# Repeating softmax denominators by DMA and moving residual sums into a wait, in a fused attention and expert kernel

## The reference

```python
x = x + attn(layernorm(x))          # c_kv = x@W_DKV; k = c_kv@W_UK; v = c_kv@W_UV; q = x@W_UQ
                                    # ctx = softmax(causal(q k^T / 4)) v ; ctx @ W_O
h = layernorm(x)
logits = h @ Wr / temp; topw, topi = top_k(logits, 2); topw = softmax(topw)
for e in range(8):
    a, g = split(h @ W1[e] + b1[e]);  y = a * silu(g) @ W2[e] + b2[e]
    out += y * sum(where(topi == e, topw, 0))
x = x + out
```

## Time and profile before

| what | us |
|---|---|
| median of 3 runs | 1150.02 (1148.51 to 1151.36) |
| the profiled execution | 1161.29 |
| its span, first to last instruction | 1159.5 |
| PE busy, in the span | 1044.3 (90%) |
| DVE busy | 762.8 (66%) |
| ACT busy | 503.1 (43%) |
| POOL busy | 411.0 (35%) |

### The profile page before, as it was taken

One profiled execution on the slowest core, in us unless ns is written; L12 is line 12 of the kernel. 1 busy time (PEld: TensorE's weight loads), 2 busy tenths in 40 slices (PEclk: granted clock), 3 DMA queues, 4 the chain that ended last, 5 costly groups with the idle time before them and its releaser, 6 DMA issues. The chain is left out here.

```text
span 1159.5 us, 19495 instructions
## 1 busy us (share of the span) xinstructions
PE 1044.3 (90%) x5364; PEld 549.1 (47%) x5365; DVE 762.8 (66%) x2270; ACT 503.1 (43%) x1060; POOL 411.0 (35%) x781
## 2 busy tenths in 40 slices
PE   5998999999999999999877730899999999999995
PEld 2443333333333333335546630466666666666663
DVE  3776999999999898896435432455555555555552
ACT  2553377777777777775343330122222222222221
POOL 5566233333333333342263345022222222222222
PEclk9997599999999999999797755899999999999998
DMA  2869766665555444414238573122222222222222
GB/s 88 261 229 264 140 129 131 133 131 129 120 120 121 85 84 85 84 41 123 92 102 299 193 234 110 35 45 46 47 45 45 45 45 45 45 45 45 45 45 27
DMA packets 102395, 121.22 MB, mean 105 GB/s; under 512 B 26352, under 2 KB 81776, under 8 KB 102320
## 3 DMA queue, kind: packets, MB, share of 16 engines
q1 hardware_dynamic: 89024, 102.55, 35.1%
q0 software_dynamic: 13296, 17.77, 9.0%
HBM read 70.27 MB, written 49.63 MB: 103 GB/s over the span
## 5 line engine op out<-in xcount | busy, mean ns | idle before, releaser
L740 ACT ACTIVATE b_prob<-bank 128x512 f32<-128x512 f32 (+3 forms) x768 | 312.8, 507 | 91.2 <-PE bank L784 90.7
L766 PE MATMUL bank<-b_k_st,b_q_st 96*128 96x512 bf16 (+3 forms) x768 | 255.6, 346 | 5.5 <-DVE b_neg_max L694 1.7
L694 DVE CUSTOM_DVE_ANT_0 bank<-bank,b_mask_max 128x256 f32<-128x256 f32 (+3 forms) x512 | 241.2, 507 | 24.5 <-PE bank L766 24.4
L652 POOL TENSOR_SCALAR_AFFINE_SELECT b_prob<-b_prob 128x128 f32<-128x128 f32 x512 | 145.9, 294 | 307.1 <-ACT b_prob L740 302.4
L784 PE MATMUL bank<-b_q_st,b_k_st 99*128 99x512 bf16 (+3 forms) x768 | 245.5, 335 | 3.2 <-ACT b_prob L740 1.1
L1644 POOL DMA_INDIRECT out_dram<-e_y,e_token x71 | 110.7, 1560 | 325.0 <-DVE e_y L1698 313.7
L697 DVE TENSOR_REDUCE b_neg_max<-bank 128x1 f32<-128x512 f32 x256 | 175.6, 686 | 13.6 <-PE bank L766 11.1
L805 PE MATMUL bank<-b_prob,b_v_aug 128*32 128x512 f32 (+3 forms) x1536 | 145.8, 498 | 0.0
L1768 PE MATMUL e_y_ps<-w_sb,e_hiddenT 128*128 x568 | 134.4, 379 | 1.8 <-ACT e_hiddenT L1721 1.8
L1751 PE MATMUL e_g_ps<-w_sb,e_rowsT 128*128 x284 | 135.4, 599 | 0.4 <-issue 0.4
L1751 PE MATMUL e_a_ps<-w_sb,e_rowsT 128*128 x284 | 133.4, 592 | 0.0
(11 more groups left out here) (172 smaller groups left out, 1007.6 us busy)
## 6 DMA issues: line engine op xcount, KB each, us to landing
w_sb<-in_L_ffn_W SPq DMA_DIRECT2D x12, 1024.0 KB
e_rows<-slot_rows SPq DMA_DIRECT2D x72, 129.0 KB, 2.0
ctx_cols<-b_ctx_out SPq DMA_DIRECT2D x16, 512.0 KB
q_parts<-a_part_q SPq DMA_DIRECT2D x8, 768.0 KB, 4.0
k_parts<-a_part_k SPq DMA_DIRECT2D x8, 768.0 KB, 4.8
b_q_st<-q_parts SPq DMA_DIRECT2D x16, 384.0 KB, 4.8
b_k_st<-k_parts SPq DMA_DIRECT2D x16, 384.0 KB, 8.1
a_x<-in_L_attn_x SPq DMA_DIRECT2D x8, 512.0 KB, 5.0
```

The costliest lines, as they stand in the source:

```text
L652: nc.gpsimd.affine_select(out=prob[n % NP][:, 0:P], in_=prob[n % NP][:, 0:P], compare_op=ALU.is_ge, fill=0.0, base=0, pattern=[[1, P]], ch ...
L694: nc.vector.tensor_tensor_reduce(scores, scores, mask_max[:, HALF - width:HALF], -1.0, -MASKED, ALU.add, ALU.min, to).then_inc(max_done, 1)
L740: nc.scalar.activation(prob[n % NP][:, 0:width], prob_ps[n % NS][:, 0:width], ACT.Exp, scale=SCALE).then_inc(prob_ok, 1)
L766: nc.tensor.matmul(out[:, 0:width], q_st[g % RING][0:STACK, h, i * P:(i + 1) * P], k_st[g % RING][0:STACK, h, half * HALF:half * HALF + wi ...
```

## The change

The reciprocals are no longer repeated by matmuls. VectorE inverts the denominators of batches 0 and 1 inside its attention loop (`INVERT_AT`, in groups 9 and 13). SP stores the reciprocals to a buffer `ctx_invs` in memory (`store_inverse`) and loads them back with each head's row repeated for 16 partitions (`load_scale`, two DMAs of 512 KB for a batch). `scale_heads` reads that tile. The spread matmuls, their matrix and GpSimd's work for it are gone.

The projection of batch 0 moves to slots 5 to 11, its transposes to 20 to 28, the projection of batch 1 to 39 to 45, and three of the four pieces of batch 2's projection come to slots 56, 58 and 60. VectorE sums and takes moments of batch b + 1 after `shift(b)` and before `choose(b)`. ScalarE takes the root of batch b + 1 before it copies the rows of batch b. The second rows of batch 1 have a buffer of their own, in the room of the bias `m_b1`; all bias loads therefore wait until the second scatter of batch 1 has landed. TensorE projects all of batch 3 after the counts of batch 1.

```diff
+            if g == NQUAD:
+                route.sync_second(sp)
             if g >= 2:
                 store(g - 2)
+            if g in (8, 12, NQUAD - 1):
+                route.denominators(sp, (8, 12, NQUAD - 1).index(g))
+            if g in (11, 14):
+                route.store_inverse(sp, (11, 14).index(g))
             if g == NQUAD - 1:
                 route.sync_first(sp)
             if g == NQUAD:
-                route.sync_second(sp)
+                route.sync_third(sp)
...
-            if unit in SPREAD_AT:
-                route.spread_matrix(pool, SPREAD_AT.index(unit))
...
+            if unit in INVERT_AT:
+                route.invert(dve, INVERT_AT.index(unit))
...
+PROJECT_0 = (5, 7, 9, 11)
+TURN_0 = (20, 22, 25, 28)
+ROUTER_0 = (22, 25, 28, 30)
+COUNT_0 = 37
+PROJECT_1 = (39, 41, 43, 45)
+PROJECT_2 = (56, 58, 60)
+INVERT_AT = (9 * UNITS + PER_HALF, 13 * UNITS + PER_HALF)
+ROOT_AT = TOTAL - 12
...
+    def store_inverse(self, sp, b):
+        sp.wait_ge(self.inv_den_ok, b + 1)
+        sp.dma_start(self.dram["inv"][b * HEADS:(b + 1) * HEADS, :].rearrange("h (t n) -> (h t) n", n=P),
+                     self.inv_den[:]).then_inc(self.inv_den_st, 16)
+
+    def load_scale(self, sp, b):
+
+        sp.wait_ge(self.inv_den_st, 16 * (b + 1))
+        if b:
+            sp.wait_ge(self.heads_ok, b * SCALES)
+        for c in range(DC):
+            of = self.dram["inv"][b * HEADS + c * P // HD:b * HEADS + (c + 1) * P // HD, :]
+            sp.dma_start(self.scale[:, c, :], of.unsqueeze(1).to_broadcast([P // HD, HD, SEQ])).then_inc(
+                self.scale_in_ok, 16)
...
+        sp.wait_ge(self.v_aug_ok, NQUAD)
+        sp.dma_start(self.wo[:], w_o.rearrange("(c p) n -> p c n", p=P)).then_inc(self.small_in, 16)
         sp.wait_ge(self.prob_sc_ok, PER_QUAD * (NQUAD - 2))
+        self.load_scale(sp, 0)
         self.load_x(sp, 1)
...
     def sync_second(self, sp):
 
-        sp.wait_ge(self.proj_ok, PAIRS)
+        self.load_scale(sp, 1)
         self.load_heads(sp, 1)
         self.store_x2(sp, 0)
+        self.store_inverse(sp, 2)
+        self.load_x(sp, 2)
+
+    def sync_third(self, sp):
+
+        self.load_scale(sp, 2)
+        self.load_heads(sp, 2)
+        self.store_x2(sp, 1)
...
+        self.load_den(sp, 3)
+        self.load_heads(sp, 3)
+        self.store_inverse(sp, 3)
+        self.load_scale(sp, 3)
+        self.load_x(sp, 3)
+        self.store_x2(sp, 2)
+        for f in range(1, FC):
+            load_w2(f)
...
+        self.store_x2(sp, 3)
+
+        sp.wait_ge(self.second_in_slot, 16 * BT * 2)
+        for e in range(EXPERTS):
+            for n in range(2):
+                sp.dma_start(self.bias[n][:, e, :], b_dram[n][e:e + 1, :].to_broadcast(
+                    [P, b_dram[n].shape[1]])).then_inc(self.loaded, 16)
...
         scale_heads(0)
         residual(0)
         moments(0)
-        invert(1)
+        self.invert(dve, 2)
...
+        scale_heads(1)
         first_normalise()
         choose(0)
         slots(0)
-        scale_heads(1)
+        residual(1)
+        moments(1)
+        scale_heads(2)
         for b in range(1, BATCH):
-            residual(b)
-            moments(b)
+            shift(b)
+            if b == 1:
+                self.invert(dve, 3)
             if b + 1 < BATCH:
-                invert(b + 1)
-            shift(b)
-            if b + 1 < BATCH:
-                scale_heads(b + 1)
+                residual(b + 1)
+                moments(b + 1)
             choose(b)
+            if b == 1:
+                scale_heads(3)
             slots(b)
...
+        for t in range(len(PROJECT_2), PAIRS):
+            self.project(pe, 2, t)
         for b in range(1, BATCH):
-            if b + 1 < BATCH:
-                for k in range(SPREADS):
-                    self.spread_out(pe, b + 1, k)
...
             self.counts(pe, b)
-            if b + 1 < BATCH:
-                for t in range(PAIRS // 2, PAIRS):
-                    self.project(pe, b + 1, t)
+            if b == 1:
+                for t in range(PAIRS):
+                    self.project(pe, 3, t)
```

More of the change, by code:

```diff
@@ L852 @@
 PAIRS = BT // 2
-SPREADS = DC * SEQ // CHUNK
+SCALES = DC * SEQ // CHUNK
 BIG = 3.0e38
[L857 to L865, removed]
+PROJECT_0 = (5, 7, 9, 11)
[4 more added lines that the diff above has]
+PROJECT_2 = (56, 58, 60)
+NARROW = [(kind, b, t) for kind, b in (("project", 0), ("turn", 0), ("project", 1)) for t in range(PAIRS)]
+INVERT_AT = (9 * UNITS + PER_HALF, 13 * UNITS + PER_HALF)
+ROOT_AT = TOTAL - 12
 POWER_AT = TOTAL - 6
@@ L873, in __init__ @@
     def __init__(self, nc, life, early, freed, low, bias, banks, dram, x, w_o, w_r, temp, b_dram, w2, w2_sb, loaded,
-                 out):
+                 second_row, out):
         def sem(name):
@@ L1019, in store_x2, with denominators @@
                      self.x2[b % 2][:]).then_inc(self.x2_st[b % 2], 16)
+    def denominators(self, sp, b):
+        for p in range(2):
+            sp.wait_ge(self.ctx_st[p], 32 * 2 * (b + 1))
+        self.load_den(sp, b)
     def sync_first(self, sp):
         _, w_o, w_r, temp, _, _ = self.sources
-        for p in range(2):
-            sp.wait_ge(self.ctx_st[p], 32 * 4)
-        self.load_den(sp, 0)
-        self.load_den(sp, 1)
         sp.wait_ge(self.prob_sc_ok, PER_QUAD * (NQUAD - 3))
@@ L1193, in wide @@
             return ap.unsqueeze(2).to_broadcast([P, ap.shape[1], n])
-        def invert(b):
-            dve.wait_ge(self.den_in_ok[b % 2], 16 * (b // 2 + 1))
-            if b:
-                dve.wait_ge(self.spread_ps_ok, b * SPREADS)
-            nc.vector.reciprocal(self.inv_den[:], self.den_in[b % 2][:]).then_inc(self.inv_den_ok, 1)
         def scale_heads(b):
             dve.wait_ge(self.heads_in_ok, 16 * (b + 1))
-            for k in range(SPREADS):
-                half = self.heads[:, k % DC, k // DC * CHUNK:(k // DC + 1) * CHUNK]
-                dve.wait_ge(self.spread_ps_ok, b * SPREADS + k + 1)
-                nc.vector.tensor_tensor(half, half, self.spread_bank(b, k)[:], ALU.mult).then_inc(self.heads_ok, 1)
+            dve.wait_ge(self.scale_in_ok, 16 * DC * (b + 1))
+            for k in range(SCALES):
+                half = slice(k // DC * CHUNK, (k // DC + 1) * CHUNK)
+                nc.vector.tensor_tensor(self.heads[:, k % DC, half], self.heads[:, k % DC, half],
+                                        self.scale[:, k % DC, half], ALU.mult).then_inc(self.heads_ok, 1)
         def residual(b):
```

149 lines of the change are left out of this document (55 added, 94 removed).

## The result

| what | us |
|---|---|
| after, median of 7 runs | 1157.34 (1155.46 to 1164.93) |
| before, median of 7 runs beside it | 1150.06 (1148.51 to 1151.36) |
| ratio of after to before | 1.0071, 95% interval 1.0048 to 1.0094 |
| profiled execution of after, its span | 1164.93, 1163.0 |

The change makes the kernel 0.7% slower; the interval of the ratio lies wholly above 1. I had forecast 1130 us with a range of 1119 to 1144, and slower at 7 in 100.

The account below looks back on a forecast made before the run. TensorE bounds attention and the experts, VectorE's serial chain the stretch between. The last scatter at E + 91.8 = 697.6 against 717.3 gains 19.7 us, so 1150.0 - 19.7 = 1130.3 us in the median, range 1119 to 1144.

Parts of the forecast that it names:

- E: End of attention's last product on TensorE: 599.9 us before, forecast 605.8 after, bounds 601 and 611.
- E + 25.4: Forecast start of normalising batch 2, after its second slot numbers (0.6 us later) and shift (1.0 us).
- it takes the place of the load of x of batch 1: First scale load in SP's queue: lands at 535.6, 10.9 us after issue, so the first projection opens at 537.0.
- Rival one: Scale loads with slowest dimension 8 get half the DMA engines: 1 MB in 6.6 us, +4 us, 1134 us; chance 0.20.
- At 552.8 it scales, 2.7 us, and normalises the first rows: VectorE after heads of batch 1 arrive, about 6 us with issue and landing; the first transpose comes at 556.4.
- my 1 us for that: Allowance for TensorE's lower clock after its longer idle at slot 5, putting the first transpose at 557.4.
- On data that SP stores, reloads and delivers by about E + 15: Scale of batch 3, ready for four multiplications of 2.7 us put between batch 1's logits and first slots.
- a difference of 20 us shrinks by 0.2 us by that, which I ignore: Profiled execution 1161.29 us against median 1150.02, 1% less; the 19.7 us gain was carried over to the median whole.
- The sums are off the chain: VectorE's sums and moments of the next batch hide in the logits' wait, costed at nothing; otherwise up to 6 us.
- rival five: Late bias loads, 5.2 MB, hold up the experts' start and make the kernel slower, some 1165 us; chance 0.07.
- The tail of 10.2 us: From the last scatter's end to the experts' first transpose, 10.2 us, kept unchanged.
- Rival three: GpSimd becomes the bound after attention, no losses and E near 602: gain 30 us, 1120 us; chance 0.13.

Follow-up runs that it names:

- e6: The changed kernel, unchanged, profiled a second time; 1156.50 us.
- e7: Changed kernel with scale loads of 16 rows each read 8 times, one loaded copy, and scale_heads(1) behind first_normalise() on VectorE; 1135.23 us, ratio to before 0.9867.
- e1: Changed kernel with the scale load's source laid out as 16 rows each read 8 times instead of 8 rows each 16 times; 1144.21 us, ratio to before 0.9941.
- e4: Loads alone, no attention or experts: pairs of 512 KB in five source shapes; 4.5 us for 128 plain rows, 10.7 to 11.0 for 8 rows repeated 16 times.
- e8: Changed kernel with only scale_heads(1) moved behind first_normalise() on VectorE; 1151.14 us, ratio to before 1.0002.
- e5: The kernel before, unchanged, profiled a second time; 1150.67 us.
- e9: Changed kernel with 16-row scale loads and one loaded copy, all four projections of batch 2 after the last product; 1138.72 us, ratio to before 0.9902.
- e11: e7 with scale_heads(3) behind slots(1) on VectorE and no pieces of batch 2's projection before the last product; 1136.44 us, ratio to before 0.9873.
- e13: e7 unchanged, run again in a held-up set beside e14; 1159.93 us, ratio to before 0.9974.
- e14: e7 without the three pieces of batch 2's projection between the last scores, beside e13; 1158.31 us, ratio to before 0.9972.
- e3: Kernel before, spread matmuls kept, with only the new order: next batch's sums and moments before choosing, its projection before this batch's transposes; 1152.90 us, ratio 1.003.
- e15: e7 with the three loads of W2 moved behind the scatters of batch 2; 1157.02 us, ratio to before 0.9964.
- e17: e7 unchanged, run a third time, in a held-up set; 1157.16 us, ratio to before 0.9957.
- e12: e7 without the three pieces of batch 2's projection between the last scores, in a held-up set; 1156.70 us, ratio to before 0.9938.

## Why the prediction was wrong

The forecast of 1130 missed by 27.3 us. By the second profiles, e6 against the forecast's instants, the parts are 10.8 of baseline, 14.6 of the chain (722.42 against 697.6 + 10.2 = 707.8), and 1.9 of rounding and spread between executions. The steps of the sum agree with their terms to 0.2 us (E + 25.4 is 25.2 by them), which changes nothing.

| instant | forecast | e6, the change | e7, mended |
|---|---|---|---|
| first projection | 537.0 | 543.8 | 535.5 |
| first transpose | 557.4 | 572.5 | 555.1 |
| last product E | 605.8 | 616.0 | 603.6 |
| first slots of batch 1 | E + 23.6 = 629.4 | E + 33.7 = 649.7 | E + 25.6 = 629.2 |
| experts' first transpose | 707.8 | 722.4 | 701.7 |

**The step that failed first: "it takes the place of the load of x of batch 1, which ... landed 10.9 us later at the soonest, at 535.6; the same bytes are ahead of it".** The bytes were right, the rate was not. The pair of scale loads keeps the DMA engines at half their share, and the first projection was 6.8 us late (e6). e1 and e4 show it: 13 to 14 us back by changing the shape. Rival one was this mechanism at 4 us. Its size was wrong: I took 6.6 us per MB, where the stretch in 585 to 594 gives 8.3 and e4 10.7 to 11.0 with issue and landing; and I let it act on the first projection and the last scaling only, not on the heads queued behind the second scale load.

The DMA share is 0.52 in these loads, 0.53 and 0.50 in e4 with a slowest dimension of 8, 0.99 there with 16 rows. The Trainium skill, "DMA: Bandwidth & Descriptors" (Rules for kernel authors, "Use all 16 engines"), says that an outermost dimension below 16 confines a DMA to at most that many engines; the trace agrees, as far as a mean over the engines can tell. The rule's direction was right; what I did with it, giving it 0.20 and 4 us, was not.

**"At 552.8 it scales, 2.7 us, and normalises the first rows": heads in 6 us.** The first transpose was 15.0 us late (e6), not 6.8. The four pieces of the first projection took 12.3 us from their start at 543.83 to the issue of heads(1) at 556.10, where I had 9.8: after an idle time of 11.27 us the first ran for 3.75 us instead of 1.89, at the clock of 0.50, and my 1 us for that was too little. Even in e7, where the idle time is 3.22 us, it takes 3.75, with a granted clock of 0.50 in 535.5 to 539.3. That is 2.5 more. Then heads(1) landed 13.15 us after its issue, not 6, since the second scale load had gone out 2.1 us ahead of it: 7.1 more. Scaling and normalising took 1.4 less than I gave them. SP's wait for the last row maxima, behind the late projection, had kept that scale load back until then; I never asked who else was behind that wait. The order on VectorE made it count for batch 0 (e8, 6.2 us). Slots between absorbed 5 us, so E was 10.2 late.

**"On data that SP stores, reloads and delivers by about E + 15".** It came at E + 27.5 (643.43 in e6): 9.1 us of waiting ahead of the first slots, nearly all of the 10.1 by which those are late. The fourth pair is only issued at 630.19, E + 14.2, once the store of the reciprocals has landed, and takes 13.2 us from there. So my E + 15 was too early even for a fast load: in e7, with 16 rows and one copy, it comes at E + 19.3 (622.89), and 0.9 us of waiting is left.

**The baseline: "a difference of 20 us shrinks by 0.2 us by that, which I ignore".** The profiled execution of before was not 1% longer all over; its 11 us lay in batches 2 and 3, in just the waits that the sum was to win back. A second profile (e5) has the experts start at 716.70. So of the 19.7 us foreseen 10.8 were not there in ordinary runs: even with every load on time this sum should have given 1141, inside my range; it is the late loads that took the time out of it. (e7 is below that since its late batches lose less, see below.)

**What was right.** The sums are off the chain, but more narrowly than I had it. Those of batch 2 ended with the logits of batch 1 in e7 (618.2 both) and 3.8 us after them in e6, where only the later scale load covered that; those of batch 3 left a wait of 2.9 us in both. The bias loads bind nothing (rival five). The tail of 10.2 us held: 712.3 to 722.4 in e6. Rival three's mechanism is true of the second half: GpSimd runs without a gap (62.6 us in e6, where I had 68.2), so the late batches lost 5.6 us less than I gave them. And in e7 the chain up to the first slots is the forecast's within 2.4 us. Part of that is luck: e7 gets there with half the bytes and another order on VectorE, and its E is 2.2 us early where its slots are 2.0 late against E. With the bytes that I had counted (e1) the first projection is still 2.1 us late.

**The third part**, three pieces of batch 2's projection ahead of the last product, is worth nothing that e9, e11 or e13 with e14 can measure. e3 is slower for another reason: its projection of batch 2 has to wait for denominators and spreads.

The best version, e7, is 1.3% faster than before in a quiet set and 0.3 to 0.4% faster in a held-up one; the change as made is 0.7 and 1.4% slower.

## What to carry to other kernels

Price a load by its shape, not its bytes: a source whose slowest dimension is 8 kept the DMA engines at half their share here (123 to 141 GB/s alone, against 232 with 16 rows and 382 with 128), and a layout that makes it 16 was worth 13 us. Before the sum is made against a profiled execution, find where its difference to the median lies; if it lies in the waits that the change removes, it is not gain. And put nothing that waits for the next batch's data ahead of work of this batch in an engine's or queue's order: here that was 6.2 us.

## What the runs showed that I had not expected

In three sets of six, TensorE's signals seem to reach ScalarE and VectorE late in batches 2 and 3 (in e15 once in batch 1 too, by 3.08 us): in e17 by 7.62, 5.77 and 3.72 us before ScalarE's copies, at the same places within some 2 us in e12 and e13, though TensorE's records have the transposes done (at 639.2 for the first of them in e17). VectorE reads the logits of batch 3 at 685.34 in e17, 7.4 us after the last router matmul. In the other three sets no profile has such a wait. It isn't the chip (sets 1, 3 and 4), and it doesn't go with the loads of W2 (e15). The large ones all lie where GpSimd issues scatters or has just ended a set (629.86 to 650 and 662.6 to 683 in e17; in the first profile of before at 679.00 and 686.05), and the new order, with its turning all under scatters, loses twice as much. That is where they stand, not what causes them, since quiet sets have the same scatters; the cause is open, and I tried nothing more on it.

A full DMA share is not yet the full rate: in e4 a pair from 16 rows read 8 times takes 6.6 to 6.9 us, one row read 128 times 5.1 to 5.3, 128 rows read once 4.5. Which property of the source costs the 2 us is open.
